# Recurrent block: another order of VectorE and TensorE work, and two identity products

## The reference, cut to what matters

```python
t = rmsnorm(x, norm1_w)
xb = einsum('bsd,de->bse', t, Wx)
xb = causal_depthwise_conv(xb, conv_w, conv_b)      # 4 taps along the sequence
r = sigmoid(xb @ Wa); i = sigmoid(xb @ Wi)
a = exp(-8 * softplus(lam) * r)
b = sqrt(maximum(1 - a * a, 1e-12)) * (i * xb)
h = scan(h[s] = a[s] * h[s-1] + b[s])
yb = gelu(t @ Wy)
h1 = x + (h * yb) @ Wo
u = rmsnorm(h1, norm2_w)
y = h1 + (gelu(u @ Wg) * (u @ Wu)) @ Wd             # 128 -> 512 -> 128
x = layernorm(x + y)
```

## Time and profile before

| | us |
|---|---|
| runs, median of 3 | 4149.69 (4143.78 to 4152.22) |
| the profiled execution | 4148.88 |
| its span, first to last instruction | 4147.1 |
| steady part of the recurrent block, ten slots | 3324.31 to 3562.12 |
| whole recurrent block, about | 3235 to 3630 |

### The profile page before, as it was taken

How to read it: one execution, slowest core, us unless ns; L and a number is a source line. 1 busy time by engine, 2 the same in 40 slices (tenths; PEclk the granted TensorE clock), 3 DMA queues, 4 the chain that set the end, 5 groups by cost and what they waited for, 6 DMA issues and landing times. The chain is left out here.

```text
span 4147.1 us, 135892 instructions
## 1 busy us (share of the span) xinstructions
PE 3616.0 (87%) x47928; PEld 2678.3 (65%) x47928; DVE 3219.3 (78%) x7754; ACT 2220.0 (54%) x4048; POOL 1737.7 (42%) x2905
## 2 busy tenths in 40 slices
PE   8996887797999998999987939999989578779986
PEld 6774666465777775777766627777744344457764
DVE  7996995255998886889973579999967677679975
ACT  4665771344444444667862446668843454445543
POOL 4667974646431111223545423332222344345544
PEclk9998995898999998999986969999999788989988
DMA  2002213696000001110005810001112000000001
GB/s 79 28 26 79 64 54 105 185 259 171 17 13 2 0 1 36 42 43 19 16 20 169 242 42 15 14 23 34 33 50 57 8 0 0 1 26 24 23 11 41
DMA packets 306791, 214.81 MB, mean 52 GB/s; under 512 B 51664, under 2 KB 285136, under 8 KB 306384
## 3 DMA queue, kind: packets, MB, share of 16 engines
q1 hardware_dynamic: 246704, 162.31, 13.5%
q0 software_dynamic: 12288, 25.19, 2.0%
q10 hardware_dynamic: 47520, 23.60, 1.9%
HBM read 127.08 MB, written 54.53 MB: 44 GB/s over the span
## 5 line engine op out<-in xcount | busy, mean ns | idle before, releaser
L2473 POOL TENSOR_TENSOR L1a_rs<-L1a_ag,eps 128x1 f32<-128x1 f32 x64 | 13.0, 203 | 397.1 <-DVE L1a_ag L2638 397.1
L703 ACT ACTIVATE L2a_PT<-L2a_psP 128x512 f32<-128x512 f32 x256 | 138.9, 595 | 63.9 <-PE L2a_psP L624 63.6
L755 DVE TENSOR_REDUCE L1x_mx<-L1x_psS 128x16 f32<-128x1024 f32 x128 | 155.9, 1218 | 16.4 <-PE L1x_psS L578 15.7
L1533 DVE TENSOR_TENSOR L0f_G<-L0f_SG,L0f_psH 128x512 f32<-128x512 f32 x106 | 73.0, 689 | 120.1 <-ACT L0f_SG L1277 74.4
L755 DVE TENSOR_REDUCE L2a_mx<-L2a_psS 128x16 f32<-128x1024 f32 x128 | 156.3, 1221 | 10.9 <-PE L2a_psS L578 8.9
L703 ACT ACTIVATE L1x_PT<-L1x_psP 128x512 f32<-128x512 f32 x256 | 138.9, 594 | 44.8 <-PE L1x_psP L624 44.3
L1114 POOL DMA_INDIRECT L0f_sorted_x<-X,L0f_IDX x128 | 123.1, 962 | 93.7 <-DMA L0f_sorted_x<-X,L0f_IDX 35.5
L774 DVE TENSOR_TENSOR L1x_PR<-L1x_psS,L1x_mx 128x1024 f32<-128x1024 f32 x128 | 156.3, 1221 | 6.3
L774 DVE TENSOR_TENSOR L2a_PR<-L2a_psS,L2a_mx 128x1024 f32<-128x1024 f32 x128 | 156.0, 1218 | 4.2
L639 PE MATMUL L1x_psB<-VB,L1x_PT 128*64 128x18 f32 x4096 | 141.0, 212 | 0.3 <-DVE L1x_ON L789 0.3
L639 PE MATMUL L2a_psB<-VB,L2a_PT 128*64 128x18 f32 x4096 | 141.0, 212 | 0.3 <-DVE L2a_ON L789 0.3
(11 more groups left out here) (622 smaller groups left out, 11763.0 us busy)
## 6 DMA issues: line engine op xcount, KB each, us to landing
L0f_WB<-in_w12a SPq DMA_DIRECT2D x53, 312.0 KB, 3.2
L0f_XB<-L0f_sorted_x SPq DMA_DIRECT2D x53, 256.0 KB
L0f_sorted_y<-L0f_YB ACTq DMA_DIRECT2D x53, 256.0 KB, 4.0
L1m_WB<-in_w12b SPq DMA_DIRECT2D x37, 321.0 KB, 4.0
L1m_XB<-L1m_sorted_x SPq DMA_DIRECT2D x37, 256.0 KB
L1m_sorted_y<-L1m_YB ACTq DMA_DIRECT2D x37, 256.0 KB, 4.3
L0x_VS<-in_ctx SPq DMA_DIRECT2D x64, 128.0 KB, 2.8
KB<-L1x_QK SPq DMA_DIRECT2D x256, 32.0 KB, 1.8
```

The costliest lines, as they stand in the source:

```text
L703: nc.scalar.activation(PT[:, A.par, 4 * hb:4 * hb + 4, :], psP[:, hb], ACT.Copy).then_inc(S[done].sem, 1)
L755: nc.vector.tensor_reduce(heads4(mx[:, T.par, :].unsqueeze(2))[:, :, :, 0], psSH, AX, ALU.max).then_inc(S["maxed"].sem, 1)
L1533: nc.vector.tensor_tensor(G[0:f, J % 2, c, :], SG[0:f, c, :], up, ALU.mult).then_inc(S["g_ready"].sem, 1)
L2473: nc.gpsimd.tensor_tensor(rs[:, A.par, 0:1], ag[:, A.par, 1:2], eps[:, 0:1], ALU.add).then_inc(S["var_eps"].sem, 1)
```

## The change

Three edits, all in the recurrent block, in every slot. On TensorE, behind the Wy product, two products of the identity with XT are written to psK, the bank of the back products, whose result is read by nothing; they wait until VectorE has read the residual of batch E out of psK. The fourth hidden pair moves ahead of the mix products. On VectorE the floor of A2 moves from behind the residual to between the second and third tap, and gating products 0 and 1 move from behind the scan and behind the product with YB to ahead of the row statistics.

```diff
--- before.py
+++ after.py
@@ -2211,7 +2211,12 @@
                             made(pe, "gates_out", B.b)
                             nc.tensor.matmul(psY, Wm("L3Wy"), XT[:, B.u, :], start=True, stop=True).then_inc(S["yb"].sem, 1)
                         if A.ok:
+                            if E.ok:
+                                made(pe, "res", E.b + 1)
+                            for _ in range(2):
+                                nc.tensor.matmul(psK[:, :], ident, XT[:, A.u, :], start=True, stop=True)
                             hidden(A, 2)
+                            hidden(A, 3)
                         if R_.ok:
 
                             made(pe, "hy", R_.b + 1)
@@ -2221,8 +2226,6 @@
                             for j in range(TB):
                                 m = nc.tensor.matmul(psT[:, j * P:(j + 1) * P], HS[:, R_.u, j * P:(j + 1) * P], Wm("L3Wo"), start=True, stop=True)
                             m.then_inc(S["mix"].sem, 1)
-                        if A.ok:
-                            hidden(A, 3)
                         if B.ok:
 
                             made(pe, "conv", 5 * (B.b + 1))
@@ -2305,8 +2308,15 @@
                         if B.ok:
                             made(dv, "xb", B.b + 1)
                             nc.vector.tensor_copy(XP[:, B.u, :, CK - 1:], seqs(psX)).then_inc(S["conv"].sem, 1)
-                            for k in range(CK):
-                                tap(B, k)
+                            tap(B, 0)
+                            tap(B, 1)
+                        if R_.ok:
+
+                            made(dv, "a2_out", R_.b + 1)
+                            nc.vector.tensor_scalar(A2[:, R_.u, :], A2[:, R_.u, :], 1.0, -1e-12, ALU.subtract, ALU.min).then_inc(S["floored"].sem, 1)
+                        if B.ok:
+                            tap(B, 2)
+                            tap(B, 3)
                         if N.ok:
                             mean_square(N, SQ1, "squares", ms, "means")
                         if E.ok:
@@ -2315,10 +2325,11 @@
                             nc.vector.tensor_tensor(RB[:, E.u], rows4(psK[:, :]), H1[:, E.u], ALU.add).then_inc(S["res"].sem, 1)
                         if R_.ok:
 
-                            made(dv, "a2_out", R_.b + 1)
-                            nc.vector.tensor_scalar(A2[:, R_.u, :], A2[:, R_.u, :], 1.0, -1e-12, ALU.subtract, ALU.min).then_inc(S["floored"].sem, 1)
                             made(dv, "a_out", R_.b + 1)
                             nc.vector.memset(seqs(A1[:, R_.u, :])[:, :, 0:1], 0.0).then_inc(S["cut"].sem, 1)
+                        if A.ok:
+                            gated(A, 0)
+                            gated(A, 1)
                         if E.ok:
                             made(dv, "res", E.b + 1)
                             row_stats(E, RB, st, ag)
@@ -2330,14 +2341,10 @@
                             made(dv, "cut", R_.b + 1)
                             made(dv, "mix", R_.b - 1)
                             nc.vector.tensor_tensor_scan(HS[:, R_.u, :], A1[:, R_.u, :], A2[:, R_.u, :], 0.0, ALU.mult, ALU.add).then_inc(S["scanned"].sem, 1)
-                        if A.ok:
-                            gated(A, 0)
                         if R_.ok:
                             made(dv, "scanned", R_.b + 1)
                             made(dv, "yb_out", R_.b + 1)
                             nc.vector.tensor_tensor(HS[:, R_.u, :], HS[:, R_.u, :], YB[:, R_.u, :], ALU.mult).then_inc(S["hy"].sem, 1)
-                        if A.ok:
-                            gated(A, 1)
                         if A.ok:
                             gated(A, 2)
                         if R_.ok:
```

## The result

| | before | after |
|---|---|---|
| runs, median of 4 | 4146.73 us | 4114.05 us (4108.05 to 4116.16) |
| the profiled execution, its span | 4148.88, 4147.1 | 4116.16, 4114.3 |
| granted clock, mean of the span | 0.927 | 0.937 |
| the block | 395.72 us | 366.13 us |
| its ten steady slots | 237.81 | 209.60 |

The ratio of the runs is 0.9918, with an interval of 0.9906 to 0.993: the change saves 34 us, 29 to 39. The forecast was 4128, its range 4113 to 4145, so the time is inside the range and 14 us under the forecast. As a saving the miss is larger: the forecast took 21.7 us off the 4149.69 of the runs known then, and the medians of the table are 32.7 us apart.

A forecast was written before the change was run, and what follows sets the result against it. No engine was full; a loop of waits bound the slots. From 4148.9, ten slots' gain of 22.2 and +1 at the edges gave 4127.7; with 0.8 for the median 4128.5, forecast 4128, range 4113 to 4145 us.

The forecast's parts named there:

- The stall and its cause: Steady slots: TensorE's wait before the third pair, for the first gating product, 39.0 us over ten slots, would nearly go.
- The new slot is 20.91: Steady slot, summed along TensorE's work, h1 and UN: 20.91 us, a gain of 2.87 if the clock stays up.
- UN follows 5.42 after h1: VectorE, end of the slot: the next UN comes 5.42 us after h1, a term taken from the old trace.
- The identity products are themselves on TensorE's path and spend 1.72 us: TensorE behind Wy: the two products use 1.72 us of what the earlier gating product frees, hidden only if HS is late.
- It stands on TensorE's path, which bounds the new slot, so nothing covers it: Down products behind the new idle place before UN's transposes: a clock fall there costs the slot 1.62 us.
- I take 0.65, two slots in five: Price of clock falls before UN's transposes: 0.65 us per slot, between 0 and 1.62; slot 21.56, gain 2.22.
- The early ones gain a few tenths ... I take +1: Edge slots: early ones gain a few tenths, last two pay 1.72 us each; +1 us, bounds -3 and +4.
- Nearly all of it is the clock: Steady slot's 2.87 us gain: mostly from the clock staying up, as an old-order slot with it up took 21.05 us.
- A: Rival: the clock never falls at the new idle place; slots 20.91 us, time 4122, chance 0.22.
- B: Rival: the clock falls in every slot and VectorE's taps are dear; slots 23.03 us, time 4143, chance 0.15.
- C: Rival: VectorE is held as long as before, by the floor's stall or the Gelu; time 4149, chance 0.05.
- D: Rival: slower, clock stays low from before UN's transposes through the identity products; slots 24.4 us, time 4158, chance 0.07.

The follow-up runs named there:

- products alone: Kernel before plus the two identity products between the Wy product and the third hidden pair, order unchanged; ratio to before 0.9928, block 368.73 us.
- order alone: Changed kernel without its two identity products; ratio to the kernel before 0.9931, block 361.72 us.
- rows split: Changed kernel, VectorE writing two of batch G's rows behind the fourth gating product and two behind the second mean square; ratio to before 0.9901, block 356.84 us.
- best less one product: Changed kernel, rows written in two halves, no identity products except four ahead of UN's transposes in the last two slots; ratio to before 0.9897, block 350.94 us.
- three joined: Changed kernel, fourth pair behind mix, rows written in two halves, identity products only ahead of UN's transposes, four in the last two slots; ratio to before 0.9986, block 374.59 us.

## Why the prediction held in its mechanism, and where it failed

Three terms of the sum were mis-sized, all to the same side: the share of cold slots (0.65 us a slot taken, 0.32 measured, 3.3 us over the ten), UN behind h1 (5.42 taken, 5.16 measured, 2.6 us) and the edges (+1 taken, -1.3 measured, 2.3 us). One step had the wrong mechanism: the identity products do not spend 1.72 us on the path of the slot; taking them away gives at most 0.1 us a slot.

**The stall and its cause: right.** TensorE no longer waits at the third pair, the pair and the mix run at full clock, the floor stalls VectorE (0.57 us, 0.8 was said), and TensorE waits ahead of UN's transposes instead. From UN = 3408.07 (3428.72 less the slot of 20.65) the rows give Wy's end at 9.1, the products' end at 10.8, the mix at 14.25 and h1 at 15.5; the prediction had 9.1, 10.8, 14.3 and 15.5.

**"The new slot is 20.91": right by its way, 0.26 too long.** All of it is the term "UN follows 5.42 after h1", taken from the earlier trace rows. It is 5.16 now. Two more rows of the kernel before, of the slot of the earlier trace rows, show what the 5.42 had in it:

```profile
3448.29 1.43 PE L2172 MATMUL L3a_psH<-L3a_UT,L3a_WG 128*128 128x512 f32 x2
...
3451.33 0.69 DVE L2285 TENSOR_TENSOR L3a_G<-L3a_GG,L3a_psH 128x512 f32<-128x512 f32 x1 [0.17 <-ACT L3a_GG L2239]
```

The fourth pair began at half clock (1.43 us, 1.02 at full clock), its Gelu came late, and the fourth gating product behind the rows waited 0.17 us for it. The place of the pair is not the reason: with the pair behind the mix but at full clock UN follows h1 by 5.16 us too, in the products alone as well as in the kernel with the fourth pair back behind the mix. So a part of what the half clock cost had been carried into the new slot, whose other terms are at full clock. Ten slots: 2.6 us.

**"The identity products are themselves on TensorE's path and spend 1.72 us": failed.** Two paths meet at the mix, and they tie. TensorE's work ends at 14.25; HS is ready at 13.98 and 14.10 in turn. Without the products the mix starts at 14.04 and 14.16 and the slot is 20.53 and 20.65 in turn, so they cost at most 0.1 us of 20.65 and not 1.72. The prediction had HS "between 13.5 and 14.75" and took TensorE's 14.3; that the number came out is in part luck, since the middle of the range for HS gives nearly the same. VectorE was earlier than the dear end because the two taps behind the floor took 2.31 us and not 3.28.

**"It stands on TensorE's path, which bounds the new slot, so nothing covers it": right in what it costs, for another reason.** A cold slot costs 1.5 to 1.6 us, because the cold back products delay VectorE as well: in the cold slot of the order alone it waits 1.79 us for the Gelu.

**"I take 0.65, two slots in five": the frequency was twice too high.** Two of ten slots were cold, at some 1.6 us each (22.19 and 22.28 less 20.65): the price of one was right. 3.2 us instead of 6.5. The cold stretch came where the prediction put it, ahead of UN's transposes. The idle time there was 1.65 us where 2.2 was expected: 0.3 of it moved ahead of Wx (1.16 us, 0.85 was expected), and UN itself came 0.26 sooner. The reason that the prediction had for a smaller share, a shorter wait, is not borne out: waits of 1.65 us went with one and two cold slots of ten, waits of 1.14 us with three (rows split) and four (best less one product). Why it was two stays open.

**"The early ones gain a few tenths ... I take +1": failed, by 2.3 us.** The start and the two early slots gained 6.3 us. The early slots, from third pair to third pair, took 21.63 and 21.05 us before and 19.38 and 19.36 after. The first of them began at half clock; the second ran at full clock before and still gained 1.7 us, and the products alone leave it at 21.05: there the gain is the order's. What went is the third pair's idle time itself (2.72 us in the earlier trace rows). "Nearly all of it is the clock" compared the new slot, 20.91, with this old one, 21.05; but this one has no rows out on VectorE, which take 1.88 us in a steady slot. For the steady slots the sentence was right: in the old order at full clock (the products alone) they take 21.12 to 21.24, so 2.6 of the 3.1 us of a warm slot are the clock's.

The late slots lost 5.0, about as much as the 3.44 of bare products and a little more would have been, but not by them: with the order alone they are as long, 63.84 us against 64.17. Where no Wx and no gates stand between mix and UN, TensorE idles 4.10 us (2.72 in the earlier trace rows) and comes out cold (6.01 us at 3555.27). The old order was cold there too (5.36 in the earlier trace rows), but then waited for the third pair anyway, and the cold stretch lay in that wait. In the new order nothing covers it: 22.51 us from mix to mix where it was 19.75. The prediction saw "no cold stretch to save" in the last slots, although have one there. With two products ahead of UN's transposes the back products are at full clock there, and the same slot takes 20.11.

**The sum.** Forecast by the profiled execution 4127.7; less 2.6 for UN, 3.3 for the clock, 2.3 for the edges, 0.2 of rounding, is 4119.3. The profiled run of after took 4116.16; the 3.2 left lie outside the block (3.9 ahead and -0.7 behind), where no instruction changed, and are the run's own. The median of the runs is 2.1 lower still.

**The identity products.** The prediction had them "spend 1.72 us of what the earlier gating product frees", on TensorE's path. In the steady slots they are hidden behind VectorE but for at most 0.1 us; but beside them two slots are cold instead of one, and at both ends of the block they lie bare. The whole block is 4.4 us longer with them. That in the old order they alone would have taken most of the gain was not considered.

**The rivals.** A (4122, the clock never falls) was nearer to the time than the forecast, and wrong in its mechanism: the clock does fall. It was near because the terms for UN and the edges had the same sign. B, C and D did not happen; C's stall exists (0.57 us for the floor, 0.17 for the Gelu) and is too small to matter. The gating products moved without the floor show C's size if it does: VectorE's 2.58 us, and a slower kernel.

**The rule on gaps.** The rows said first that the clock may fall behind 2.72 us of idle time or not the earlier trace rows. Now it fell behind 1.65 us (after) and 1.14 us (best less one product), and most gaps of the same lengths left it up; with the products alone gaps of 1.64 to 2.03 us ahead of the third pair, one in each of the ten slots, all left it up. The Trainium skill ("TensorE: Matmul & The Clock Gate", section "Why this matters for your kernels") asks only that long idle gaps between bursts be avoided. By that rule alone no steady slot of the changed kernel would be cold; two are, so the measurement goes against it here. The same page of the Trainium skill (section "A second HAM failure mode: psum-queue depth-cycling") tells of a clock that swings where TensorE is idle briefly but often. That agrees with the cold slots here, which have 1.16 and 1.65 us in each, but not with the products alone, where TensorE idles three times a slot and the granted clock is 1.00 over the ten slots. Which of several small gaps matters isn't settled by the runs; that filling one of them suffices is.

## What to carry to other kernels

When a stall is removed from a loop, look for the engine that ties with the one you followed, and re-read the terms behind it too: 5.42 had a wait in it that came from the half clock and went with it. Price warm slots by themselves before giving all of a gain to the clock. Products that fill idle time belong where the idle time is after the change, and only as many as fit; behind a stall that is gone they are dead weight, and an instruction moved ahead needs its producer moved as well.

## What was not expected of the hardware

- The clock fell behind idle stretches of 1.14 us (back products 5.30 us instead of 3.74), although 2.72 us had left it up in the same block before, and 2.6 to 2.7 us ahead of the mix left it up in seven of ten slots of the three joined.
- It fell at the same slots in both traces of the changed kernel: the second, of a later series of runs, had its cold back products at the same places, 4.82, 5.32, 5.96 and 4.96 us against 4.85, 5.37, 6.01 and 4.99. The whole block repeats to 0.1 us, while the program around it differs by 3%.
- A single 512-column product (two MATMULs, 0.86 us) in a gap that leaves idle stretches of 0.85 and 0.29 us around it keeps the clock up in every slot, where the two gaps without it, 0.85 and 1.14, do not.
